# First attention of a two-layer network: queries stacked with their squares, and steps placed anew

## Chip, core and metric

The kernel runs on one core of a Trainium2 chip. The metric is the device time of one execution in microseconds, compared by the median of several runs.

## What is computed

Two layers, each an attention and a feed-forward with a residual and a layer norm after either. Only the first attention is touched, beside two placements at the end of the first feed-forward. It is a linear attention with random features over 4 batches of 2048 rows, 16 heads of 16:

```python
proj = einsum('bhld,md->bhlm', x, orf) / d_k ** 0.25          # x is q or k, m = 64
norm = sum(x * x, axis=-1, keepdims=True) / (2 * sqrt(d_k))
phi  = (exp(proj - norm) + 1e-6) / sqrt(64)
kv, ksum = einsum('bhlm,bhld->bhmd', k_phi, v), sum(k_phi, axis=2)
out  = (q_phi @ kv) / (q_phi @ ksum)
x    = layernorm(x + out @ Wo.T + bo)
```

The feed-forward after it quantizes its weights and its inputs to 4 bits in blocks of 16; the weights are prepared during the first attention. A softmax attention and a routed feed-forward follow, unchanged.

## The kernel before

`make_plan` writes one list of steps. Each engine's program walks through this list and takes the steps that it has a function for, in the list's order; semaphores hold it where it needs another engine's result. Each engine is thus an in-order queue, and where a step stands in the list sets what it waits behind.

**Data.** The 8192 rows are 16 chunks C of 512 rows, 4 per batch b. For a chunk of keys the steps are k (two products with halves ht of 128 columns of Wk), v, phi (features of the keys, 4 per chunk) and kv (sums over the rows, 16 per batch); at the end of a batch kvs and kvt turn the sums into the matrices kvV and kvD (four copies on VectorE, L1467 to L1470). k of the next batch waits for these copies (`dve_kvt`).

**Queries** (`queries_order`): q(C, ht) is a product of 4 records, whose result ScalarE writes to qT with the bias (L1239); GpSimd squares it into q2 (L1800). pq(C, ht, g) makes the features of 4 heads in two banks: for k in 0, 1 a product of 32 rows of Wblk (the random features) with qT, and then for k in 0, 1 a product of 32 rows of Nblk (-1/8 for each head's block) with the squares, added in the same banks. ScalarE takes the exponential (L1248) and GpSimd adds 1e-6 and scales (L1805). The text calls that instruction the epsilon. num(C, ht) makes denominators in bank 7 and numerators in bank 4; VectorE takes the reciprocal (L1481) and multiplies into aT (L1486). o(C, g) is the output product, which VectorE adds to the residual X (L1493). res(C) is GpSimd's addition of the output bias to X (L1780). st0 takes the statistics (L1418, L1422), GpSimd makes rstd of them (L1813, L1815), and ap0 applies the norm (four instructions, L1429).

**Order.** The keys of batch 0 run alone (`keys_order(0)`), then the queries of batch b beside the keys of batch b + 1 (`beside_queries`, which puts so many key units behind each query step, 12 for a chunk). In the last batch there are no keys: two streams of queries, chunks 12 and 14 and chunks 13 and 15, alternate, and a third prepares the first two input groups of the feed-forward (`inputs_order`: qx, a quantization on VectorE; xa on ScalarE; xb, four instructions over 1024 columns on GpSimd, L1862 to L1869). The second stream has its own banks and buffers (`way`).

**Weights** (`weights_order`) of the feed-forward, for each of three matrices m: wl loads it, wq quantizes (five VectorE instructions over up to 1536 columns), wa (ScalarE) and wb (three of VectorE) round, and six wt transpose on TensorE through bank 7, which num and o also use. 81 steps with their blanks, one beside each query step.

**End of the feed-forward.** While its last tiles run, the first maxima (M on TensorE into two banks, MR a reduction on VectorE of 1.16 us, L1574) of the softmax attention are taken; 32 of them make row (0, 0), from which scores can start. The load xc2 (step pl, SP's queue) brings rows for the preparation of batch 1, whose transposes (pt) stand on TensorE's queue among the maxima.

In the records of TensorE all products have line L744 and all transposes L747. A float32 product leaves two records per instruction.

Of the kernel before, what the change touches and what calls it, by code (L numbers as in the profile page):

```python
# [12 lines left out]
ALU = mybir.AluOpType  # L13
# [48 lines left out]
def queries_order(b, chunks, way):  # L62
    stats = None
    for c in chunks:
        C = 4 * b + c
        yield [("q", C, 0)]
        yield [("q", C, 1), ("fq", C)]
        for ht, g in ((0, 0), (0, 1), (1, 0)):
            yield [("pq", C, ht, g)]
        yield [("num", C, 0)] + ([("ap0", stats)] if stats is not None else [])  # L70
        yield [("pq", C, 1, 1)]
        yield [("num", C, 1), ("res", C)]
        yield []
        for g in range(2):
            yield [("o", C, g)] + ([("st0", C)] if g else [])
        stats = C
    yield []
    yield [("ap0", C)]


def beside_queries(plan, b, keys, weights):

    behind = {"q": (1, 2), "pq": (1, 1, 1, 2), "num": (0, 3), "o": (1, 0)}
    for units in queries_order(b, range(4), 0):
        plan += units + next(weights, [])
        for name, C in (u[:2] for u in units if u[0] in behind):
            at = sum(u[:2] == (name, C) for u in plan)
            for _ in range(behind[name][at - 1]):
                plan += next(keys, [])

# [17 lines left out]
def inputs_order(G):  # L108

    for step in (("qx", G), ("xa", G), ("xb", G, 0), ("xb", G, 1), ("xb", G, 2), ("xb", G, 3)):  # L110
        yield [step]
        yield []
# [108 lines left out]
def make_plan():  # L221
# [57 lines left out]
    together(plan, queries_order(3, (0, 2), 0), queries_order(3, (1, 3), 1), chain(inputs_order(0), inputs_order(1)))  # L279
# [13 lines left out]
    for T in range(-1, NT + 7):  # L293
# [23 lines left out]
        if T == NT + 3:  # L317
            plan.append(("ap1", NT - 8))
        if T == NT:
# [17 lines left out]
    plan += [("pl", 1, 0), ("phase2",)]  # L337
# [113 lines left out]
def program(nc, t, ctx):  # L451
# [73 lines left out]
    qT = [take(f"qT{i}", [P, 2, 512]) for i in range(2)]  # L525
    q2 = take("q2", [P, 2, 512])
# [8 lines left out]
    way = ({"q2": q2, "rB": rB, "phq": phq, "banks": (4, 5, 7)},  # L535
           {"q2": k2[0], "rB": phi[1][:, 512:1024], "phq": vq, "banks": (0, 1, 3)})
# [125 lines left out]
    for e, o in enumerate((0, 8192, 24576, stack_at, 4096, 12288, 16384, 28672)):  # L662
# [27 lines left out]
    (pool_setup, pool_res, pool_k2, pool_phi, pool_q, pool_pq, pool_eps, pool_eps1, pool_rstd, pool_shift, dve_wr, pool_qx,  # L690
     pool_ps, pool_R2, pool_at) = (sem(n) for n in (
        "pool_setup", "pool_res", "pool_k2", "pool_phi", "pool_q", "pool_pq", "pool_eps",
# [47 lines left out]
    def tensor_program(eng):  # L740
# [102 lines left out]
        def q(C, ht):  # L843
# [3 lines left out]
            if ht:  # L847
                w.wait_ge(act_q, at["q", C, 0])
# [9 lines left out]
        def pq(C, ht, g):  # L858
            i, (b4, b5, b7) = C % 2, way_of(C)["banks"]
            w.wait_ge(act_q, at["q", C, 1])  # L860
            w.wait_ge(dve_setup, 4)
# [8 lines left out]
            w.wait_ge(pool_q, at["q", C, 1])  # L870
            for k in range(2):

                s, c = slice(32 * (2 * g + k), 32 * (2 * g + k) + 32), slice(P * (2 * g + k), P * (2 * g + k) + P)
                mm(bank(b5 + k), Wblk[s, c], qT[i][s, ht, :], True, False)
            for k in range(2):
                s, c = slice(32 * (2 * g + k), 32 * (2 * g + k) + 32), slice(P * (2 * g + k), P * (2 * g + k) + P)
                d = mm(bank(b5 + k), Nblk[s, c], way_of(C)["q2"][s, ht, :], False, True)
            d.then_inc(pe_pq, 1)

        def num(C, ht):  # L880
# [20 lines left out]
            else:  # L901
                w.wait_ge(act_q, at["q", C, 1])
# [270 lines left out]
    def scalar_program(eng):  # L1173
# [59 lines left out]
        def q(C, ht):  # L1233
# [5 lines left out]
            eng.activation(qT[C % 2][:, ht, :], bank(b4), ACT.Identity, bias=bqk["q"][:, ht:ht + 1], scale=1.0).then_inc(act_q, 1)  # L1239
# [157 lines left out]
    def vector_program(eng):  # L1397
# [34 lines left out]
        def setup():  # L1432
# [5 lines left out]
            eng.memset(W[:, 1280:1536], 0.0).then_inc(dve_setup, 1)  # L1438

# [20 lines left out]
        def kvt(b):  # L1460
# [9 lines left out]
            eng.tensor_copy(Dn[64:128, :, 16:32], kv[64:128, :, 16:32]).then_inc(dve_kvt, 1)  # L1470

# [287 lines left out]
        stages = {"setup": setup, "wq": wq, "wb": wb, "bo": bo, "kvt": kvt, "num": num, "o": o, "st0": st0,  # L1759
# [8 lines left out]
    def pool_program(eng):  # L1768
# [23 lines left out]

        def q(C, ht):
            w.wait_ge(act_q, at["q", C, ht])
            if former(C) is not None:
# [446 lines left out]
```

## Time and profile before

| | us |
|---|---|
| median of 3 runs | 4654.1 |
| their range | 4651.65 to 4659.11 |
| the profiled execution | 4639.76 |
| its span | 4637.7 |
| TensorE busy in the span | 4385.2 (95%) |
| VectorE busy | 3396.8 (73%) |
| ScalarE busy | 2794.6 (60%) |
| GpSimd busy | 1012.4 (22%) |

PE is TensorE's products, PEld its weight loads, DVE is VectorE, ACT ScalarE, POOL GpSimd, SP the engine that issues most DMAs. PEclk is the mean granted clock of TensorE as a share of its full speed. A row of the timeline has the start, the length, the engine, the line, the operation with output and inputs, a count, and in brackets how long the engine stood idle before it and for whom. The first attention takes the first 690 us of the span, the first feed-forward lasts until 1340 us.

### The profile page before, as it was taken

What the parts mean: (1) busy time and instruction counts of PE and PEld (TensorE: products, weight loads), DVE (VectorE), ACT (ScalarE), POOL (GpSimd) and SP (SyncE); (2) the same over time, 40 slices, a digit from 0 to 9 for tenths busy, and PEclk for the clock granted to TensorE, in tenths of its full rate; (3) what the DMA queues carried; (4) which work ended last, traced back from release to release, by engine and by line L of the source; (5) the groups of instructions that cost most, each with busy time, mean ns of one, the idle gap of its engine ahead of it and who ended that gap; (6) DMA issues with size and microseconds to landing.
All of it is one profiled execution on the core that took longest, in us unless ns stands there. A gap on an engine that the chain in (4) does not pass through costs nothing.

```text
span 4637.7 us, 66610 instructions
## 1 busy us (share of the span) xinstructions
PE 4385.2 (95%) x26073; PEld 1670.4 (36%) x26076; DVE 3396.8 (73%) x3722; ACT 2794.6 (60%) x5273; POOL 1012.4 (22%) x989
## 2 busy tenths in 40 slices
PE   9988979999979999999999999999999999999895
PEld 5544536666642222222222222222222232222285
DVE  1443368877977788888778888777888988888332
ACT  3332323333326788887777778777777767787621
POOL 3443453445311200001121010221111001000223
PEclk9999989999989999999999999999999999999998
DMA  3111000021213321122332311333222122222232
GB/s 103 34 34 55 19 20 5 28 73 62 103 53 95 105 93 42 65 77 72 113 105 72 98 57 71 119 95 110 63 77 83 46 72 59 73 77 77 74 116 54
DMA packets 230278, 330.52 MB, mean 71 GB/s; under 512 B 36870, under 2 KB 171464, under 8 KB 227912
## 3 DMA queue, kind: packets, MB, share of 16 engines
q1 hardware_dynamic: 227084, 318.40, 20.9%
q0 software_dynamic: 2880, 7.87, 0.9%
q8 instruction: 205, 3.36, 0.3%
q14 instruction: 109, 0.89, 0.1%
HBM read 218.71 MB, written 98.04 MB: 68 GB/s over the span
## 4 chain that ended last, share of the span: by engine, by line
PE 67%; DVE 11%; POOL 3%; DMA 2%; issue 2%; ACT 1%; SPq 1%; POOLq 0%; DVEq 0%; another core or an unknown queue 0%; ACTq 0%
PE ps L744 66%; DVE mx L1574 4%; PE ps L747 2%; DVE stat L1418 1%; DMA pk<-Ob 1%; DVE hn L1412 1%; DVE hn L1553 0%; DVE hn L1548 0%; DMA KS<-kd 0%; DMA rd<-pk 0%; SPq L2058 0%; DVE eb L1429 0%; DMA QS<-mrow 0%; DMA ypar<-eo,tabs 0%; ACT Pb L1340 0%
## 5 line engine op out<-in xcount | busy, mean ns | idle before, releaser
L1574 DVE TENSOR_REDUCE mx<-ps 128x1 f32<-128x1024 f32 x2048 | 2407.4, 1219 | 434.3 <-PE ps L744 431.1
L1340 ACT ACTIVATE Pb<-ps 128x512 f32<-128x512 f32 x4096 | 2202.4, 597 | 521.0 <-PE ps L744 516.8
L744 PE MATMUL ps<-QS,KS 98*128 98x512 bf16 x4096 | 1249.4, 386 | 15.6 <-ACT Pb L1340 7.4
L744 PE MATMUL ps<-Pb,VA 128*32 128x512 f32 x8192 | 1096.9, 608 | 0.1
L744 PE MATMUL ps<-KM,QM 64*128 64x512 bf16 x4096 | 658.1, 388 | 48.5 <-DVE mx L1574 46.7
L744 PEld LDWEIGHTS ps<-QS,KS 98*128 98x128 bf16 x4096 | 260.2, 98 | 1087.7 <-ACT Pb L1340 904.4
L744 PEld LDWEIGHTS ps<-KM,QM 64*128 64x128 bf16 x4096 | 179.9, 93 | 603.9 <-issue 351.8
L744 PEld LDWEIGHTS ps<-Pb,VA 128*32 128x32 f32 x8192 | 161.4, 108 | 400.5 <-issue 399.5
L1887 POOL CAST mrow<-mres 16x128 bf16<-16x128 f32 x64 | 17.9, 279 | 1293.0 <-ACT mres L1177 1293.0
L1481 DVE RECIPROCAL rB<-ps 128x512 f32<-128x512 f32 x28 | 94.0, 3356 | 262.0 <-PE ps L744 261.7
L744 PE MATMUL ps<-wdT,hT 128*128 128x256 f32 (+1 forms) x768 | 194.3, 395 | 15.6 <-DVE X L1559 14.2
L744 PE MATMUL ps<-wgT,xqT 128*128 128x352 f32 x512 | 170.2, 477 | 0.0
L1820 POOL TENSOR_TENSOR den<-Ob,den 128x512 f32<-128x512 f32 x64 | 81.4, 1272 | 396.4 <-DMA den<-rd 396.4
L744 PEld LDWEIGHTS ps<-wdT,hT 128*128 128x128 f32 (+1 forms) x768 | 141.2, 193 | 68.5 <-issue 42.8
L744 PE MATMUL ps<-wuT,xqT 128*128 128x352 f32 x512 | 161.9, 459 | 0.0
L1813 POOL TENSOR_SCALAR vpe<-mv 128x4 f32<-128x4 f32 (+1 forms) x52 | 14.9, 286 | 607.9 <-DVE mv L1422 607.7
L1876 POOL CAST parts<-pres 128x1024 bf16<-128x1024 f32 x32 | 37.6, 1176 | 460.6 <-ACT pres L1177 431.1
L1198 ACT ACTIVATE phi<-ps 128x1024 f32<-128x1024 f32 x64 | 65.5, 1024 | 119.3 <-PE ps L744 119.3
L1532 DVE TENSOR_TENSOR hh<-ps,sg 128x704 f32<-128x704 f32 x64 | 56.5, 882 | 92.7 <-PE ps L744 88.4
L1177 ACT ACTIVATE pres<-ps 128x512 f32<-128x512 f32 x64 | 38.1, 597 | 132.2 <-PE ps L744 110.2
L744 PEld LDWEIGHTS ps<-wuT,xqT 128*128 128x128 f32 x512 | 97.6, 191 | 54.6 <-issue 0.7
L1248 ACT ACTIVATE phq<-ps 128x1024 f32<-128x1024 f32 x56 | 57.3, 1023 | 98.5 <-PE ps L744 98.5
(238 smaller groups left out, 4415.7 us busy)
## 6 DMA issues: line engine op xcount, KB each, us to landing
QM<-qd SPq DMA_DIRECT2D x128, 256.0 KB
KM<-kd SPq DMA_DIRECT2D x128, 256.0 KB
qd<-parts SPq DMA_DIRECT2D x96, 256.0 KB, 2.8
kd<-parts SPq DMA_DIRECT2D x96, 256.0 KB, 2.8
QS<-qd SPq DMA_DIRECT2D x64, 384.0 KB
KS<-kd SPq DMA_DIRECT2D x64, 384.0 KB
vdr<-vst SPq DMA_DIRECT2D x64, 256.0 KB, 2.8
den<-rd SPq DMA_DIRECT2D x64, 256.0 KB
```

What stands on the lines that cost most here:

```text
L744: return eng.matmul(out, a, b, start=start, stop=stop, skip_group_check=skip)
L747: return eng.transpose(out, a, ident[0:n, 0:n])
L1177: return eng.activation(out, a, ACT.Copy, bias=0.0, scale=1.0)
L1198: eng.activation(phi[n % 3], bank(1, 2), ACT.Exp, bias=0.0, scale=1.0).then_inc(act_phi, 1)
L1248: eng.activation(flat(way_of(C)["phq"][ht][:, 2 * g:2 * g + 2, :]), bank(b5, 2), ACT.Exp, bias=0.0, scale=1.0).then_inc(act_pq, 1)
L1340: eng.activation(Pb[(u - 1) % 9], o, ACT.Exp, bias=0.0, scale=0.25).then_inc(act_A, 1)
L1412: eng.tensor_tensor(blk(xn), blk(x), wide(rs, n // 16, 16), ALU.mult).then_inc(own, 1)
L1418: d = eng.bn_stats(stat[:, i % 4, j, :], x[:, j, :])
L1481: eng.reciprocal(f["rB"], bank(b7)).then_inc(dve_rec, 1)
L1532: eng.tensor_tensor(hh[p % 2][:, 704 * b:704 * b + 704].rearrange("p (a b) -> p a b", a=2), bank(2, 2).rearrange("p (a b) -> p a b", a=2)[ ...
L1574: eng.tensor_reduce(mx4[qc % 2][:, 4 * i + q, h:h + 1], o, AX, ALU.max).then_inc(dve_D, 1)
L1820: eng.tensor_tensor(den, Ob, den, ALU.mult).then_inc(pool_at, 1)
```

## The change

- The query matrix and its bias are permuted on the host, so that a product's result has the heads of group g = 0 and g = 1 in alternating blocks of 32 partitions. ScalarE writes it twice, to qs[0] and qs[1]; VectorE then overwrites in each the 32-partition blocks of the other group with squares (128 instructions in all). A matrix Wq4, built at the start by eight copies on VectorE, holds the matching rows of Wblk and Nblk. pq is then two products of 64 rows. GpSimd's squares, q2 and their semaphores go.
- `queries_order`: ap0 of a chunk stands with the next chunk's pq(C, 0, 0), also from one batch to the next, and only in the last batch at the end; res stands with pq(C, 0, 1).
- Weights: their steps begin at the thirteenth step of the keys of batch 0 and run on beside the queries, except behind the first num of a chunk. w0 and bo move up.
- `inputs_order` loses its blanks.
- The load pl(1, 0) moves ahead of the end of the feed-forward, and preparation steps start only when 12 maxima are in the list.

```diff
-        for ht, g in ((0, 0), (0, 1), (1, 0)):
-            yield [("pq", C, ht, g)]
-        yield [("num", C, 0)] + ([("ap0", stats)] if stats is not None else [])
+        yield [("pq", C, 0, 0)] + ([("ap0", stats)] if stats is not None else [])
+        yield [("pq", C, 0, 1), ("res", C)]
+        yield [("pq", C, 1, 0)]
+        yield [("num", C, 0)]
         yield [("pq", C, 1, 1)]
-        yield [("num", C, 1), ("res", C)]
+        yield [("num", C, 1)]
...
-    yield []
-    yield [("ap0", C)]
+    if b == 3:
+        yield []
+        yield [("ap0", C)]
...
-    for units in queries_order(b, range(4), 0):
-        plan += units + next(weights, [])
+    for units in queries_order(b, range(4), 4 * b - 1 if b else None):
+        plan += units
...
+        if not units or units[0][0] != "num" or units[0][2]:
+            plan += next(weights, [])
...
     for step in (("qx", G), ("xa", G), ("xb", G, 0), ("xb", G, 1), ("xb", G, 2), ("xb", G, 3)):
         yield [step]
-        yield []
...
-    together(plan, keys_order(0))
-    plan.append(("bo",))
     plan.append(("w0",))
+    for i, units in enumerate(keys_order(0)):
+        plan += units + (next(w, []) if i > 11 else [])
+        if i == 11:
+            plan.append(("bo",))
...
-    together(plan, queries_order(3, (0, 2), 0), queries_order(3, (1, 3), 1), chain(inputs_order(0), inputs_order(1)))
+    together(plan, queries_order(3, (0, 2), 11), queries_order(3, (1, 3), None), chain(inputs_order(0), inputs_order(1)))
...
+        if T == NT + 4:
+            plan.append(("pl", 1, 0))
...
-    plan += [("pl", 1, 0), ("phase2",)]
+    plan.append(("phase2",))
...
-        if len([u for u in plan if u[0] == "M"]) % 2 == 0 and ("mx", 0, 0) not in plan:
+        made = len([u for u in plan if u[0] == "M"])
+        if made % 2 == 0 and made > EARLY + 2 and ("mx", 0, 0) not in plan:
             background()
...
             if ht:
-                w.wait_ge(act_q, at["q", C, 0])
+                w.wait_ge(act_q, 2 * at["q", C, 0])
...
-            w.wait_ge(pool_q, at["q", C, 1])
+            w.wait_ge(dve_q2, 2 * at["q", C, ht] - 1 + g)
             for k in range(2):
 
-                s, c = slice(32 * (2 * g + k), 32 * (2 * g + k) + 32), slice(P * (2 * g + k), P * (2 * g + k) + P)
-                mm(bank(b5 + k), Wblk[s, c], qT[i][s, ht, :], True, False)
-            for k in range(2):
-                s, c = slice(32 * (2 * g + k), 32 * (2 * g + k) + 32), slice(P * (2 * g + k), P * (2 * g + k) + P)
-                d = mm(bank(b5 + k), Nblk[s, c], way_of(C)["q2"][s, ht, :], False, True)
+                d = mm(bank(b5 + k), Wq4[64 * k:64 * k + 64, g, :], qs[i][g][64 * k:64 * k + 64, ht, :])
...
-            eng.activation(qT[C % 2][:, ht, :], bank(b4), ACT.Identity, bias=bqk["q"][:, ht:ht + 1], scale=1.0).then_inc(act_q, 1)
+            for g in range(2):
+                eng.activation(qs[C % 2][g][:, ht, :], bank(b4), ACT.Identity, bias=bqk["q"][:, ht:ht + 1], scale=1.0).then_inc(act_q, 1)
...
+            w.wait_ge(ld_n, 16)
+            w.wait_ge(dve_setup, 4)
+            for j in range(4):
+                s, c = slice(32 * j, 32 * j + 32), slice(P * j, P * j + P)
+                eng.tensor_copy(Wq4[s, j % 2, :], Wblk[s, c])
+                d = eng.tensor_copy(Wq4[s, 1 - j % 2, :], Nblk[s, c])
+            d.then_inc(dve_blk, 1)
...
+        def q(C, ht):
+            for g in range(2):
+                w.wait_ge(act_q, 2 * at["q", C, ht] - 1 + g)
+                for k in range(2):
+                    o = 64 * k + 32 * g
+                    x = qs[C % 2][g][o:o + 32, ht, :]
+                    d = eng.tensor_tensor(qs[C % 2][g][64 * k + 32 - 32 * g:64 * k + 64 - 32 * g, ht, :], x, x, ALU.mult)
+                d.then_inc(dve_q2, 1)
...
-        def q(C, ht):
-            w.wait_ge(act_q, at["q", C, ht])
-            if former(C) is not None:
-                w.wait_ge(pe_pq, at["pq", former(C), 1, 1])
-            else:
-                w.wait_ge(pe_phi, 64 if C else 0)
-            x = qT[C % 2][:, ht, :]
-            eng.tensor_tensor(way_of(C)["q2"][:, ht, :], x, x, ALU.mult).then_inc(pool_q, 1)
```

## Rows read from the trace of the kernel before

**Rows 1.** Windows of batches 1 to 3: length, busy us (count) by engine, PEclk, DMA share, GB/s.
```profile
249.10:420.70 171.60, 154.71 (x1240) 83.99 (x1238) 63.50 (x92) 53.68 (x69) 68.66 (x60) 0.96 0.17 54
420.70:579.90 159.20, 148.21 (x1219) 81.05 (x1220) 54.82 (x86) 48.91 (x57) 64.34 (x60) 0.99 0.07 21
579.90:690.00 110.10, 84.07 (x352) 39.22 (x350) 66.12 (x89) 23.54 (x26) 56.15 (x43) 0.81 0.03 11
```

**Rows 2.** Groups by shape, 0 to 690 us: count, busy us, mean ns, idle before.
```profile
L744 PE MATMUL ps<-q,Nblk 32*128 32x512 f32 x224 | 60.5, 617 | 0.0
...
L1805 POOL TENSOR_SCALAR phq<-phq 128x1024 f32<-128x1024 f32 x56 | 58.4, 1043 | 110.3 <-ACT phq L1248 110.3
```

**Rows 3.** Waits: TensorE from 86 us (us, times, longest); last row VectorE from 0.
```profile
PE ps L744 <- DVE kvD L1470: 13.1, 3, 4.6
...
PE ps L747 <- DVE rB L1481: 6.7, 4, 2.6
...
DVE kvV L1467 <- PE ps L747: 74.2, 1, 74.2
```

**Rows 4.** Timeline, batch 1: start us, us, engine, line, operation, count, idle before.
```profile
400.46 0.60 PE L744 MATMUL ps<-Nblk,k 64*128 64x256 f32 x4
...
400.89 0.60 PE L744 MATMUL ps<-Wblk,kT 64*128 64x256 f32 x4
...
401.85 1.13 PE L744 MATMUL ps<-qT,Wblk 32*128 32x512 f32 x4
...
402.81 1.02 PE L744 MATMUL ps<-q,Nblk 32*128 32x512 f32 x4
...
403.77 0.65 PE L744 MATMUL ps<-phi,va 128*32 128x64 f32 x32
```

**Rows 5.** Timeline: a query copy, the q product after it, and two-input SBUF instructions of VectorE.
```profile
339.46 0.69 ACT L1239 ACTIVATE qT<-ps,bq 128x512 f32<-128x512 f32 x1 [3.72 <-PE ps L744]
...
340.20 1.98 PE L744 MATMUL ps<-xq,WqT 128*128 128x512 f32 x4 [0.19 <-ACT qT L1239]
...
1299.83 1.63 DVE L1412 TENSOR_TENSOR hn<-hh,hs 128x1408 f32<-128x1408 f32 x1
...
588.18 1.22 DVE L1412 TENSOR_TENSOR fq<-X,fs 128x1024 f32<-128x1024 f32 x1
...
636.19 2.00 DVE L1412 TENSOR_TENSOR fq<-X,fs 128x1024 f32<-128x1024 f32 x1
```

**Rows 6.** Timeline at the end of batch 2: ap0, and TensorE after the copies.
```profile
582.64 2.09 DVE L1429 TENSOR_SCALAR X<-X,mv,rstd 128x256 f32<-128x256 f32 x4 [1.47 <-POOL rstd L1815]
...
585.99 6.42 PE L744 MATMUL ps<-xq,WqT 128*128 128x512 f32 x8 [4.57 <-DVE kvD L1470]
...
587.83 0.34 PEld L744 LDWEIGHTS ps<-xq,WqT 128*128 128x128 f32 x1 [0.52 <-issue]
```

**Rows 7.** Timeline, batch 0: the o product behind a quantization and a reciprocal.
```profile
123.46 3.38 PE L744 MATMUL ps<-WoT,aT 128*128 128x256 f32 x8 [3.26 <-DVE aT L1486]
```

**Rows 8.** Timeline, batch 3: the wait for squares, ap0 beside GpSimd's instructions.
```profile
640.22 2.08 PE L744 MATMUL ps<-qT,Wblk 32*128 32x512 f32 x4 [3.79 <-POOL q L1800]
...
664.90 4.72 POOL L1780 TENSOR_TENSOR X<-X,bo 128x1024 f32<-128x1024 f32 x2
...
665.90 8.64 DVE L1429 TENSOR_SCALAR X<-X,mv,rstd 128x256 f32<-128x256 f32 x4
...
682.09 0.76 DVE L1486 TENSOR_TENSOR aT<-ps,phi 128x256 f32<-128x256 f32 x2
```

**Rows 9.** Timeline, end of the feed-forward: last add, xc's load, and who waited.
```profile
1339.72 0.42 DVE L1559 TENSOR_TENSOR X<-ps,X 128x256 f32<-128x256 f32 x1 [1.21 <-PE ps L744]
...
1346.64 0.51 SPq L2029 DMA_DIRECT2D xc<-x1d  x1
...
1351.17 1.12 PE L747 MATMUL ps<-identity,xc 128*128 128x128 f32 x4 [10.36 <-DMA xc<-x1d]
...
1352.87 4.62 DVE L1574 TENSOR_REDUCE mx<-ps 128x1 f32<-128x1024 f32 x4 [8.63 <-PE ps L744]
```

More of the change, by code:

```diff
@@ L59, in keys_order, with queries_order @@
     yield [("kvt", b)]
-def queries_order(b, chunks, way):
-    stats = None
+def queries_order(b, chunks, stats):
     for c in chunks:
@@ L524, in program @@
     k2 = [take(f"k2{i}", [P, 2, 512]) for i in range(2)]
-    qT = [take(f"qT{i}", [P, 2, 512]) for i in range(2)]
-    q2 = take("q2", [P, 2, 512])
+    qs = [[take(f"qs{i}_{g}", [P, 2, 512]) for g in range(2)] for i in range(2)]
+    Wq4 = take("Wq4", [P, 2, P])
     va = [take(f"va{i}", [P, 4, 16, 32]) for i in range(2)]
@@ L534, in program @@
     vq = [v.rearrange("p a b c -> p (a b c)").rearrange("p (a b) -> p a b", a=4) for v in va]
-    way = ({"q2": q2, "rB": rB, "phq": phq, "banks": (4, 5, 7)},
-           {"q2": k2[0], "rB": phi[1][:, 512:1024], "phq": vq, "banks": (0, 1, 3)})
+    way = ({"rB": rB, "phq": phq, "banks": (4, 5, 7)},
+           {"rB": phi[1][:, 512:1024], "phq": vq, "banks": (0, 1, 3)})
     way_of = lambda C: way[C in (13, 15)]
@@ L859, in pq @@
             i, (b4, b5, b7) = C % 2, way_of(C)["banks"]
-            w.wait_ge(act_q, at["q", C, 1])
-            w.wait_ge(dve_setup, 4)
+            w.wait_ge(dve_blk, 1)
             if C == 0:
@@ L901, in num @@
             else:
-                w.wait_ge(act_q, at["q", C, 1])
+                w.wait_ge(act_q, 2 * at["q", C, 1])
             for k in range(4):
@@ L1757, in yn @@
             norm_apply(xr[g][:, 5 * f:5 * f + 5, :], ("yp", g, f), 5)
-        stages = {"setup": setup, "wq": wq, "wb": wb, "bo": bo, "kvt": kvt, "num": num, "o": o, "st0": st0,
+        stages = {"setup": setup, "wq": wq, "wb": wb, "bo": bo, "kvt": kvt, "q": q, "num": num, "o": o, "st0": st0,
                   "ap0": ap0, "fold": fold, "qx": qx, "up": up, "qa": qa, "qb": qb, "qc": qc, "da": da, "st1": st1,
@@ L1929, in ys @@
                     in_=xr[g][:, b, :], in_offset=None, bounds_check=8191, oob_is_err=False).then_inc(st_fin, 16)
-        stages = {"setup": setup, "res": res, "k": k, "phi": phi_, "q": q, "pq": pq, "st0": st0, "st1": st1, "st2": st2,
+        stages = {"setup": setup, "res": res, "k": k, "phi": phi_, "pq": pq, "st0": st0, "st1": st1, "st2": st2,
                   "yp": yp, "of": of, "xb": xb, "ps": ps, "oe": oe, "R2": R2, "gx": gx,
@@ L2173, in layout @@
     kt = lambda w, n: f(np.asarray(w).T.reshape(-1, P, n).transpose(1, 0, 2).reshape(P, -1))
+    mid = np.arange(D).reshape(2, 2, 2, 32).transpose(0, 2, 1, 3).reshape(-1)
     for n in "qkvo":
-        a[f"W{n}T"] = kt(inputs[f"L0_attn_W{n}"], D)
+        a[f"W{n}T"] = kt(np.asarray(inputs[f"L0_attn_W{n}"])[mid if n == "q" else slice(None)], D)
     for n in "qk":
-        a[f"b{n}"] = f(np.asarray(inputs[f"L0_attn_b{n}"]).reshape(2, P).T)
+        a[f"b{n}"] = f(np.asarray(inputs[f"L0_attn_b{n}"])[mid if n == "q" else slice(None)].reshape(2, P).T)
     a["bo"] = f(np.broadcast_to(np.asarray(inputs["L0_attn_bo"]).reshape(1, D), (P, D)))
```

4 lines of the change are left out of this document (2 added, 2 removed).

## Prediction

> **What bounds the kernel now.** I read the windows first, cut where the first query product of each batch starts [rows 1]. In the second and third batch TensorE is busy 90 and 93% of the time while VectorE, ScalarE and GpSimd are at 31 to 40%, so here TensorE's instructions are the time, plus its waits. In the last 110.1 us, which hold the fourth batch, TensorE falls to 76%, at a mean granted clock of 0.81, and VectorE is at 60%: this stretch is a chain through several engines. Then the groups by shape [rows 2]: the norm product of the queries (Nblk with the squares) has 224 records (32 more read their squares from a key buffer); it is a product of its own, as long as that of the features. Third the waits [rows 3]: TensorE for the copies of the key-value sums (kvD) 13.1 us, for a reciprocal ahead of weight transposes 6.7. Last the timeline of single places. The feed-forward stage after 690 us isn't touched but for two placements at its end.
>
> **Part 1: one product for features and norm.** One pq step starts at 401.85, its norm half at 402.81, the next unit at 403.77 [rows 4]: 0.96 us for the features, 0.96 for the norms. In either half two 32-row products, 4 records of 512 columns, run side by side. The new step has two 64-row products. Does such a pair run side by side too? The keys' products show it: 4 records of 64 rows and 256 columns in the 0.43 us from 400.46 to 400.89 [rows 4], half the columns in half the time. So a pq step costs 0.96 instead of 1.92. In the three TensorE-bound batches: 48 steps x 0.96 = 46.1 us at full clock, 47 at the mean granted clock of 0.98 [rows 1]. The last batch's 16 steps (15 us) lie in the chain and are counted in part 5. Bounds of the product: 0 (pairs in series) to 0.96 a step.
>
> **Part 2: what makes the stacked queries.** ScalarE writes each result twice: 32 more activations x 0.687 = 22 us [rows 5], on an engine a third busy. But the second query product, q(C,1), reuses the bank and waits for both copies, 0.69 us later than now. The key unit between covers it when it is a 1.9 us product (first chunk of a batch) and not when it is a small kv unit (the other three), where q(C,1) already starts on the first copy's end (340.20 after 339.46 + 0.69 [rows 5]). 9 x 0.69 = +6. The squares leave GpSimd (32 instructions, no price: it doesn't bound there) for VectorE: 128 instructions over 32 partitions. None of that form is in the trace. Two-input SBUF rows take 1.63 us for 1408 elements and 1.22 for 1024 [rows 5], a slope of 1.06 ns, so 512 elements take 0.68; the lower bound is 0.55 (by that slope alone), the upper 1.1 (the 1024 row beside GpSimd took 2.00, 1.64 times 1.22 [rows 5]). I take 0.68: 128 x 0.68 = 87 us, 5.4 per chunk of some 37. In the first three batches this is beside TensorE: a square starts when ScalarE is done, VectorE has the residual add and 1.8 us of statistics ahead of it and is then free, and pq(C,0,0) follows q(C,1) and two key units, some 5.7 us after the first copy, where the first pair of squares needs 1.4. Without that cover each chunk would pay what is left. ScalarE's second copies also stand ahead of the keys' exponentials: +1 per batch, between 0 and 2, taken as +3. The 8 block copies at the start fall where VectorE is idle.
>
> **Part 3: the norm of a batch's last chunk (ap0).** At the end of a batch VectorE does statistics, waits for GpSimd's rstd, applies the norm (2.09 us [rows 6]), and only then copies the sums; k(C,0) waits for these: TensorE is idle 4.57 us and resumes at half speed, 8 records of the query product take 6.42 us [rows 6] where 4 take 1.98 at full speed [rows 5], and a weight load of 0.34 us follows a pause of 0.52 [rows 6], 0.86 for a record of 512 columns. There are three such waits, 13.1 us together [rows 3]. With ap0 behind the next chunk's squares, the copies come right after the statistics; the wait falls from 4.6 to about 1.1, as the query product before it ends 1.1 us before the copies would. 3 x 3.5 = 10.5, and the slow clock behind it (6.42 less 3.96 is 2.5 here, about 2 on the mean) 3 x 2: -16 together. ap0 moves to where VectorE is free. What is queued behind it there is num's reciprocal, 5 us later.
>
> **Part 4: weights.** The batches with weight steps last 171.6 (second) and 159.2 us (third) [rows 1]: 12.4 us for 10 or so transposes which are 0.6 of product each; the rest is waiting. The transposes wait for the reciprocal on bank 7 (6.7 us in 4 waits [rows 3]) and for residual adds. In the first batch a quantization of 1536 columns stood ahead of a reciprocal, whereupon TensorE sat 3.26 us and then took 3.38 us for 8 records of 256 columns, half speed [rows 7]. Now a weight step is taken in 41 of the first batch's key steps, where bank 7 is free and VectorE idle (74.2 us without a break [rows 3]), and none right behind the first num. By count the whole sequence of 81 ends in batch 0. Gone: about -7 of bank waits and -5 of the aT stall; new: the third quantization lies between o(1,0) and o(1,1), whose add frees the bank of the next q, so +3. Net -9, bounds -14 and 0. The first loads (w0, the weights, bo) are issued earlier on SP's queue, ahead of some x loads; SP's next waits are for products of TensorE, so nothing late is put ahead. bo's product now stands at key step 11, whose turn comes long after the loads at the start: no price. The x add of GpSimd (res, 2.36 us each, 4.72 for two [rows 8]) moves behind pq(C,0,1)'s epsilon, ahead of pq(C,1,0)'s: that one is needed two units later, no price.
>
> Parts 1 to 4: -47 + 6 + 3 - 16 - 9 = -63, with [-75, -40].
>
> **Part 5: the last batch.** Two chunks run together. From the copies to the end of the last aT (585.99 less the 0.15 of a signal [rows 6]) it takes now 97 us (682.09 + 0.76) [rows 8]. I lay the new order out by engine. Chunks 12 and 13: the input quantization (qx, then xb) has lost its blank steps, so GpSimd gets four xb (SBUF passes over 1024 columns, each about as long as a res) and two res among its epsilons (1.04 each [rows 2]); the seventh and eighth epsilon come some 22 us after the first. The first reciprocals come 2 us sooner, the last two 5 us later than now: +5. Chunks 14 and 15: GpSimd no longer owes xb or squares. The wait for squares (3.79 us [rows 8]) goes, so does most of the slow clock behind it; VectorE has 16 squares (10.9 us) and two ap0 ahead of the reciprocals. Laid end to end from the last aT of the first pair: 40 us instead of 60. But ap0 took 8.64 us beside the big GpSimd instructions [rows 8] where it takes 2.09 otherwise [rows 6], and it now falls beside res: +6. So -20 + 5 + 6 = -9, with [-20, +8].
>
> **Part 6: end of the feed-forward.** xc2 is loaded after the last x1d store, at 1346.64; TensorE is idle 10.36 us for it and VectorE 8.63 [rows 9]. The load moves to where the last dn is done (its add starts at 1339.72 [rows 9]), and lands in 4.5 us as now. Maxima go on until 12 are made before the first preparation step, so VectorE goes on from 1344.24 (1352.87 less 8.63). Row (0,0) needs VectorE for all 32 maxima, so its idle 8.63 us are the price: -9 with what the slow clock after the idle time costs, bounds -14 and -4. The preparation steps put off come later beside the main loop, which has room for them well ahead of batch 1's first use.
>
> **The sum.** -63 - 9 - 9 = -81. The profiled execution took 4639.8 us (span 4637.7 and 2.1 around it): 4559 by the sum. The median of the runs is 4654.1, 0.3% above it; the times are compared by medians, so I forecast 4654.1 - 81 = 4573.
>
> **Rivals.** (a) *The port between VectorE and GpSimd.* ap0's 8.64 us and the 2.00 for 1.22 [rows 5, 8] show that the two hold each other up on SBUF operands. Were each pair of squares to wait for one epsilon (1.04 [rows 2]), the last batch would gain nothing (+6 instead of -9) and each of 12 chunks would start 1 us later: -81 + 15 + 12 = -54, 4600 us. Chance 20%.
> The Trainium skill (SBUF — State Buffer, "SBUF: two separate sides") speaks against moving squares to VectorE: an instruction with two SBUF inputs contends with GpSimd for an exclusive lock held for the whole instruction. By that rule the squares cost up to twice; the 2.00 us row agrees with it, and (a) is its time.
> (b) *More comes back*: fewer long waits, so the clock (0.96 in the second batch) stays at 1.0, and the last batch follows the laid-out order without +6. -81 - 8 - 12, about 4553. Chance 12%.
> (c) *The pair of 64-row products doesn't overlap*: a step stays at 1.9. The 47 go and the last batch gains 5 less: 4573 + 52 = 4625. Against it speak the keys' rows [rows 4]. Chance 3%.
> (d) *Slower*: the squares are late at every chunk. They stand on VectorE's in-order queue behind the add and statistics; if pq(C,0,0) waits over 3.3 us in all 16 chunks, and a half-speed stretch of 2 us follows each as in [rows 6], the 81 are lost (16 x 5.3 = 85). With squares 6 us late: 4573 + 128 = 4701. Now the cover is 5.7 us against 1.4, so VectorE would have to be 8 us behind. Chance 4%.
> Forecast 61%.
>
> **How the numbers follow.** Forecast's own range: 4573 with parts at their ends not all together, 4548 to 4595. To hold 8 in 10 I add case (a) and most of (b): 4545 to 4612. A change within 0.2% (9 us) can't be told from none here. Faster: (a), (b), (c), the forecast: 0.93, less a little for what I can't see: 0.92; same 0.03; slower 0.05.
>
> **What would show it.** Pq records of 64 rows, 4 per 0.96 us, and no second group; three kvD waits near 1 us; squares at 0.68 us; the third batch some 18 us shorter, the second about 31 (no weights left in it); the stretch from the copies to the last aT near 88 us; no DMA wait before the first transposes of xc. Wrong would make it: squares over 1 us, TensorE waiting for squares at chunk starts, a GpSimd queue that stays behind in chunks 12 and 13, or weights that stall the keys.

## The result and the profile after

| us | before | after |
|---|---|---|
| median of the runs (4 each) | 4652.9 | 4571.0 |
| their range | 4651.3 to 4659.1 | 4567.6 to 4578.1 |
| profiled execution's span | 4637.7 | 4569.3 |
| TensorE busy | 4385.2 | 4315.6 |
| VectorE busy | 3396.8 | 3491.5 |

The ratio is 0.9824, with a 95% interval of 0.9806 to 0.9841: 82 us faster, where 81 were forecast. In a later comparison (g_after below) it was 0.9846, 0.983 to 0.9862. The profiled execution of before lies 13 us under its median and that of after on its median, so the two spans differ by 68 us only. In these traces the stretch from the first score to the last product with V varies between 2992 and 3009 us and what follows it between 235 and 255, for one and the same kernel too (the two traces of the change: 2993.8 and 246.3, 2994.3 and 235.3). In the change's two traces the stages of the attention repeat to 1.3 us, its last batch to 0.1, and the reasons are read there. Batch 1 of before is less steady: in e4_end, whose plan is the same up to there, it takes 174.9 us instead of 171.7, at a mean granted clock of 0.94 instead of 0.96.

Stages of the traces in us, cut where the first query product of a batch starts (the fourth ends where its last residual add starts; [rows 1] cut it at 579.90, where that product starts at 579.5, hence 158.7 and 109.9 here); "chain" is the part of the fourth batch from the end of the kvD copies to the end of the last aT; "end" is from the last add of the feed-forward to the first score:

| kernel | start | batch 0 | batch 1 | batch 2 | batch 3 | chain | feed-forward | end |
|---|---|---|---|---|---|---|---|---|
| before | 83.6 | 165.5 | 171.7 | 158.7 | 109.9 | 97.0 | 650.4 | 65.3 |
| after | 84.9 | 152.0 | 139.6 | 139.6 | 106.8 | 98.1 | 651.5 | 54.8 |
| e1_old_products | 83.5 | 162.3 | 153.4 | 153.4 | 104.5 | 94.1 | 648.9 | 54.9 |
| e2_ap0 | 84.5 | 164.3 | 165.9 | 153.4 | 93.6 | 83.2 | 651.5 | 65.4 |
| e3_weights | 85.3 | 164.9 | 158.7 | 159.7 | 110.3 | 97.4 | 650.4 | 63.9 |
| e4_end | 83.2 | 164.1 | 174.9 | 159.4 | 110.1 | 97.2 | 650.4 | 54.8 |

Up to the first score the change gains 75.9 us: 63.4 before batch 3, 3.1 in it, 10.5 at the end, less 1.1 in the feed-forward. The chain itself is 1.1 us longer, what lies around it in batch 3 is 4.2 shorter.

The windows of batches 1 to 3, for [rows 1]: length, busy us (count) of TensorE, its weight loads, VectorE, ScalarE, GpSimd, the granted clock, DMA share, GB/s:

```profile
236.94:376.50 139.56, 130.31 (x1154) 75.07 (x1154) 74.73 (x117) 53.05 (x65) 56.49 (x52) 1.00 0.19 61
376.50:516.10 139.60, 130.31 (x1154) 75.09 (x1155) 74.78 (x117) 53.06 (x65) 56.47 (x52) 1.00 0.08 24
516.10:622.90 106.80, 72.65 (x288) 30.50 (x288) 98.54 (x121) 27.91 (x34) 53.09 (x34) 0.82 0.03 10
```

TensorE has 18 to 24 us less to do in batches 1 and 2, and the second no longer differs from the third. In the last batch TensorE went from 84 to 73 us and VectorE from 66 to 99 of 107: VectorE is nearly always busy there. The groups by shape, for [rows 2] (busy us, mean ns | idle before):

```profile
L1492 DVE TENSOR_TENSOR qs<-qs 32x512 f32<-32x512 f32 x128 | 103.4, 808 | 22.2 <-ACT qs L1245 19.9
L754 PE MATMUL ps<-qs,Wq 64*128 64x512 f32 x256 | 74.0, 667 | 17.3 <-ACT phq L1254 10.2 <-DVE qs L1492 7.1
L1245 ACT ACTIVATE qs<-ps,bq 128x512 f32<-128x512 f32 x64 | 40.5, 684 | 91.7 <-PE ps L754 91.7
```

The waits of TensorE from 86 us on, for [rows 3] (us in total, times, longest):

```profile
PE ps L754 <- DVE X L1516: 11.0, 11, 2.9
PE ps L754 <- DVE qs L1492: 7.1, 3, 3.5
PE ps L754 <- ACT qs L1245: 6.2, 9, 0.8
PE ps L754 <- DVE kvD L1483: 4.6, 4, 1.7
```

The nine waits for the second copies are the nine of part 2, with its 6.2 us; before, eight waits of 0.2 us stood there, 1.6 in all, so the second copies cost 4.6 more. The three waits for kvD that made 13.1 us are 0.98 each; the fourth, 1.7, is in batch 0, where TensorE had none before. The timeline of a feature step in batch 1, for [rows 4], and of the start of batch 2, for [rows 6]:

```profile
390.55 1.13 PE L754 MATMUL ps<-qs,Wq 64*128 64x512 f32 x4
391.51 0.60 PE L754 MATMUL ps<-Wblk,kT 64*128 64x256 f32 x4
...
376.54 1.96 PE L754 MATMUL ps<-xq,WqT 128*128 128x512 f32 x4 [0.66 <-DVE X L1516]
379.47 1.95 PE L754 MATMUL ps<-xk,WkT 128*128 128x512 f32 x4 [0.98 <-DVE kvD L1483]
```

The step takes 0.96 us, from 390.55 to 391.51, with its norms in it. TensorE waits 0.98 us for the copies and goes on at full speed. The end of the feed-forward, for [rows 9]:

```profile
1274.39 0.36 SPq L2043 DMA_DIRECT2D xc<-x1d  x1
...
1276.59 9.24 DVE L1597 TENSOR_REDUCE mx<-ps 128x1 f32<-128x1024 f32 x8
...
1279.51 1.11 PE L757 MATMUL ps<-identity,xc 128*128 128x128 f32 x4
```

The transposes of xc no longer wait for the load, and eight maxima run without a break where VectorE stood idle 8.63 us.

### The profile page after: what moved, and what is told of

Read it like the earlier page. It is cut to its first block, busy times and chain, and to the rows that moved or that the text cites. A ratio compares the mean times of both kernels' runs of the same rounds, so it can differ in the third digit from the quotient of the medians.

```text
span 4569.3 us, 66262 instructions
## 1 busy us (share of the span) xinstructions
PE 4315.6 (94%) x25817; PEld 1642.9 (36%) x25820; DVE 3491.5 (76%) x3858; ACT 2811.9 (62%) x5305; POOL 978.9 (21%) x957
## 4 chain that ended last, share of the span: by engine, by line
PE 68%; DVE 11%; DMA 3%; POOL 2%; issue 2%; ACT 1%; SPq 1%; POOLq 0%; DVEq 0%; another core or an unknown queue 0%; ACTq 0%
PE ps L754 66%; DVE mx L1597 4%; PE ps L757 2%; DMA pk<-Ob 1%; DVE stat L1424 1%; DVE hn L1418 1%; DMA x2d<-eb 1%; DVE qs L1492 0%; DVE hn L1576 0%; DMA rd<-pk 0%; DVE hn L1571 0%; DMA KS<-kd 0%; SPq L2072 0%; DVE eb L1435 0%; DMA QS<-mrow 0%
## 5 line engine op out<-in xcount | busy, mean ns | idle before, releaser
L1504 DVE RECIPROCAL rB<-ps 128x512 f32<-128x512 f32 x28 | 94.0, 3358 | 106.8 <-PE ps L754 106.7
L754 PE MATMUL ps<-wgT,xqT 128*128 128x352 f32 x512 | 171.7, 481 | 0.0
L754 PEld LDWEIGHTS ps<-wdT,hT 128*128 128x128 f32 (+1 forms) x768 | 140.6, 192 | 68.5 <-issue 42.9
L1492 DVE TENSOR_TENSOR qs<-qs 32x512 f32<-32x512 f32 x128 | 103.4, 808 | 22.2 <-ACT qs L1245 19.9
L1182 ACT ACTIVATE pres<-ps 128x512 f32<-128x512 f32 x64 | 38.2, 598 | 132.4 <-PE ps L754 110.3
```

The costliest lines, as they stand in the source:

```text
L754: return eng.matmul(out, a, b, start=start, stop=stop, skip_group_check=skip)
L1182: return eng.activation(out, a, ACT.Copy, bias=0.0, scale=1.0)
L1492: d = eng.tensor_tensor(qs[C % 2][g][64 * k + 32 - 32 * g:64 * k + 64 - 32 * g, ht, :], x, x, ALU.mult)
L1504: eng.reciprocal(f["rB"], bank(b7)).then_inc(dve_rec, 1)
```

## The experiments

**First round: which part gives what.** Four kernels on one chip, before at 4650.4 us. The ratios aren't the quotients of the medians (these are 0.9923 for e1 and 0.9965 for e3 and e4), so the gains in time are known to some 6 us only, and the stages above say more. e1 is the change with the old feature and norm products; its edit is to put back the lines of q2, of Nblk's product and of GpSimd's q that the diff takes out:

```diff
-                d = mm(bank(b5 + k), Wq4[64 * k:64 * k + 64, g, :], qs[i][g][64 * k:64 * k + 64, ht, :])
+                mm(bank(b5 + k), Wblk[s, c], qT[i][s, ht, :], True, False)
...
+                d = mm(bank(b5 + k), Nblk[s, c], way_of(C)["q2"][s, ht, :], False, True)
```

> Every placement of the change (norms, weights, inputs, res, the load), but the queries' features and norms as two products again, squared on GpSimd. My account of the change: the placements are worth 16 (norm), 9 (weights) and 9 (end of the feed-forward), so about 34 us of the 82, 4619 us, and the stacked product some 48; the second and third batch last about 152 us each, 13 more than with the stacked product. Rival, that VectorE's squares ate the gain of the last batch (they took 1.37 us each there for 0.68): then the stretch from the last kvD copy to the last aT is shorter here, about 85 us, than the 97 that both kernels show, and the time nearer to 4607. If the squares cost nothing there, that stretch stays at 97 or more.

Measured: 4614.7 us, ratio 0.9936 (0.9916 to 0.9957), the second and third batch at 153.4. The chain, 94.1, lies between the rival's 85 and the 97 of squares that cost nothing. Stacking alone is after less e1: -10.3, -13.8 and -13.8 us in batches 0 to 2, and +2.3 in batch 3 (chain +4.0).

e2 is before with the norm placed anew and nothing else:

```diff
-        for ht, g in ((0, 0), (0, 1), (1, 0)):
-            yield [("pq", C, ht, g)]
-        yield [("num", C, 0)] + ([("ap0", stats)] if stats is not None else [])
+        yield [("pq", C, 0, 0)] + ([("ap0", stats)] if stats is not None else [])
+        yield [("pq", C, 0, 1)]
+        yield [("pq", C, 1, 0)]
+        yield [("num", C, 0)]
...
-    yield [("ap0", C)]
+    if b == 3:
+        yield [("ap0", C)]
```

> The kernel before with the norm of a chunk behind pq(C,0,0) of the next, also across batches; nothing else. My account: three waits for the copies fall from 4.6 to 1.1 us and the half-speed stretch behind each (2 us) goes, so 16 us, 4637; the third batch lasts 153 to 154 us instead of 159.2, a boundary sooner. Rival: the half speed has another cause than the wait; then 10 us, 4643, and the q products at the start of the fourth batch still run at half speed.

Measured: 4623.9 us, ratio 0.9942 (0.9923 to 0.9961), so 27 us. The starts of the batches give some 15 of them (batches 0 to 2: -1.2, -5.8, -5.3; batch 3 around its chain: -2.5), and the chain of the last batch gives 13.8 more: 2.6 up to its first reciprocal, since TensorE is no longer at half speed behind the copies (12 records of the query product take 5.39 us there instead of 8.14), 1.7 up to the first one of chunks 14 and 15, and 9.4 among the last four. VectorE's timeline shows how these come, beside the 8.64 us of [rows 8]:

```profile
620.75 4.83 DVE L1430 TENSOR_SCALAR X<-X,mv,rstd 128x256 f32<-128x256 f32 x8
637.28 3.36 DVE L1482 RECIPROCAL rB<-ps 128x512 f32<-128x512 f32 x1 [11.70 <-PE ps L745]
```

All eight norm instructions stand where VectorE has 11.7 us to spare. Before, four stood ahead of the second reciprocal and four, the 8.64 us, ahead of the third. TensorE's waits in the fourth batch of before, not read before the prediction, say what that cost:

```profile
PE ps L744 <- DVE aT L1486: 14.6, 4, 11.1
```

One wait of 11.1 us, for an aT behind the norm. In e2 the longest such wait is 3.3.

e3 is before with the weights' steps, w0 and bo placed as in the change, e4 is before with pl(1, 0) and the preparation placed as in it:

```diff
+        if not units or units[0][0] != "num" or units[0][2]:
+            plan += next(weights, [])
...
+    for i, units in enumerate(keys_order(0)):
+        plan += units + (next(w, []) if i > 11 else [])
```

> The kernel before with the weights' steps (and w0, bo) begun beside the keys of batch 0; nothing else. My account: 9 us, 4644; the second batch falls from 171.6 to about 159 us like the third, the first batch gains little since it now holds the steps of two matrices. Rival: the keys of batch 0 pay for it; then the first query product starts 5 us or more later than 83.6 us and the time is 4649 or more.

```diff
+        if T == NT + 4:
+            plan.append(("pl", 1, 0))
...
+        if made % 2 == 0 and made > EARLY + 2 and ("mx", 0, 0) not in plan:
```

> The kernel before with the load of xc2 and the first preparation steps placed as in the change; nothing else. My account: the first score product comes 55 us after the last add of the feed-forward instead of 65, TensorE doesn't wait for the load: 9 to 10 us, 4643. Rival: the preparation steps put off are paid in the main loop; then the stretch from the first score to the last V product (2992 us) is longer by as much and the time is the same as before.

Measured: e3 4634.2 us, ratio 0.9971 (0.9958 to 0.9984), batch 1 from 171.7 to 158.7 and no other stage by over 2; e4 4634.2, ratio 0.9978 (0.9964 to 0.9993), the end from 65.3 to 54.8. The main loop doesn't visibly pay for the steps put off: 2994 us in e4, 2992 before. Of e3's 13.0 us in batch 1 some 5 are the clock and not waits, by an estimate from the granted clock (0.96 of 171.7 us and 0.99 of 158.7, so 6.9 us against 1.6 lost). Against e2, e1 adds the dense input blocks and the early res to the last batch (and the weights' placement, which alone left the chain at 97.4): its chain is 94.1 against 83.2. The two placements thus take back 10.9 of the 13.8 that the norm gave, by the difference of two kernels that also differ in the weights; the third round undoes them by themselves.

**Second round: the last batch, and the squares' cover.** One run each; before took 4644.4 us on that chip. f1 puts the blanks between the input blocks back, f2 the x blocks' addition of the last batch behind num(C, 1):

```diff
     for step in (("qx", G), ("xa", G), ("xb", G, 0), ("xb", G, 1), ("xb", G, 2), ("xb", G, 3)):
         yield [step]
+        yield []
```

> The changed kernel with the blanks in the input quantization of the last batch restored; nothing else. The last batch gained nothing (98.1 us from the last kvD copy to the last aT, 97.0 before), while the moved norm alone brought it to 83.2. My theory: the close order of the inputs fills GpSimd's queue ahead of the epsilons of chunks 12 and 13; with the blanks the third reciprocal no longer comes 8 us after the second but 4, and the stretch falls to about 89 us. Rival: only the squares cost (22 us for 16 of them); then the first four reciprocals come closer but the stretch stays at 95 or more, as GpSimd's xb then meets the squares of chunks 14 and 15.

```diff
-        yield [("pq", C, 0, 1), ("res", C)]
+        yield [("pq", C, 0, 1)] + ([("res", C)] if b < 3 else [])
...
-        yield [("num", C, 1)]
+        yield [("num", C, 1)] + ([("res", C)] if b == 3 else [])
```

> The changed kernel with res of the last batch back beside num(C,1); nothing else. Theory: two res of 2.4 us stand ahead of the epsilons on which num waits; the stretch from the last kvD copy to the last aT falls by 2 to 5 us from 98.1. Rival: no change in it, since xb and the squares decide.

f4 makes the last batch's squares over one column of 512:

```diff
-                    x = qs[C % 2][g][o:o + 32, ht, :]
+                    n = 1 if C > 11 else 512
+                    x = qs[C % 2][g][o:o + 32, ht, 0:n]
```

> The changed kernel with the squares of the last batch taken over 1 of 512 columns (the rest of the squares is left out there, so the output of those chunks is not the reference's). Theory: the 16 squares of chunks 14 and 15, 22 us, are on the chain; without them the stretch from the last kvD copy to the last aT falls from 98.1 to 78 to 82 us. Rival: GpSimd's queue decides; then it stays above 90.

| kernel | time | chain | its clock | reciprocals of chunks 12 and 13 after the copies | first one of chunks 14 and 15 |
|---|---|---|---|---|---|
| after | 4571.0 | 98.1 | 0.81 | 24.3, 28.5, 36.6, 40.9 | 81.2 |
| f1_blanks | 4582.1 | 95.4 | 0.86 | 24.7, 29.0, 33.2, 37.5 | 78.5 |
| f2_late_res | 4576.4 | 93.0 | 0.87 | 23.0, 27.2, 36.6, 40.9 | 76.1 |
| f4_one_column | 4583.3 | 88.8 | 0.88 | 16.8, 21.0, 34.9, 39.1 | 71.9 |

(Before: 20.0, 24.2, 28.5, 32.7 and 70.6, at a clock of 0.80.) The times hold the loop's variation of some 10 us and can't rank these; the chains can. Each of the three gives some of it back: 2.7, 5.1 and 9.3 us. That is f1's rival (95 or more) and not its 89, f2's theory, and neither of f4's two (78 to 82, above 90). What they act on is seen in the change's own timeline, on TensorE, VectorE and GpSimd in turn:

```profile
553.23 1.94 PE L754 MATMUL ps<-phq,kvD 128*32 128x512 f32 x8 [8.78 <-POOL phq L1819]
...
582.13 6.42 PE L754 MATMUL ps<-qs,Wq 64*128 64x512 f32 x16 [3.33 <-DVE qs L1492]
592.00 2.08 PE L754 MATMUL ps<-qs,Wq 64*128 64x512 f32 x4 [3.45 <-DVE qs L1492]
...
536.10 7.05 DVE L1435 TENSOR_SCALAR X<-X,mv,rstd 128x256 f32<-128x256 f32 x4
543.18 3.36 DVE L1504 RECIPROCAL rB<-ps 128x512 f32<-128x512 f32 x1
...
574.09 21.98 DVE L1492 TENSOR_TENSOR qs<-qs 32x512 f32<-32x512 f32 x16
...
537.07 2.36 POOL L1803 TENSOR_TENSOR X<-X,bo 128x1024 f32<-128x1024 f32 x1
...
547.70 2.34 POOL L1880 TENSOR_TENSOR fq<-fc,fq 128x1024 f32<-128x1024 f32 x1
550.11 1.93 POOL L1883 TENSOR_TENSOR fq<-fq,fs 128x1024 f32<-128x1024 f32 x1
552.13 1.05 POOL L1819 TENSOR_SCALAR phq<-phq 128x1024 f32<-128x1024 f32 x1
...
576.36 2.74 POOL L1880 TENSOR_TENSOR fq<-fc,fq 128x1024 f32<-128x1024 f32 x1
579.17 2.26 POOL L1883 TENSOR_TENSOR fq<-fq,fs 128x1024 f32<-128x1024 f32 x1
```

In chunks 12 and 13 the first reciprocal comes right behind the norm of chunk 11 (536.10 to 543.15), whose four instructions take 7.05 us beside res (537.07) and its neighbours for the 1.38 that they take alone. Then TensorE waits 8.78 us for the epsilon at 552.13, which stands behind two input blocks on GpSimd's queue; f1 spreads these, and its third and fourth reciprocals come 3.4 us sooner after the copies. In chunks 14 and 15 sixteen squares take 21.98 us instead of the 10.9 of sixteen at 0.68, while GpSimd is busy 18.26 of these 21.98, with two late input blocks (576.36, 579.17) among its work.

f5 makes each square of the first three batches twice, in order, to see how much room VectorE has there:

```diff
+                    if C < 12:
+                        eng.tensor_tensor(qs[C % 2][g][64 * k + 32 - 32 * g:64 * k + 64 - 32 * g, ht, :], x, x, ALU.mult).then_inc(dve_tw, 1)
+                        w.wait_ge(dve_tw, 4 * (at["q", C, ht] - 1) + 2 * g + k + 1)
```

> The changed kernel with every square of batches 0 to 2 made twice, one after the other. My prediction's step, that VectorE's squares lie beside TensorE there: the second and third batch stay at 139.6 us (to 141), though VectorE gets 8 times 0.7 us more a chunk. Rival: the squares are on the path at the start of each chunk; then each of the batches is longer by 4 times 1.4 to 2.8 us, 145 to 151.

Measured: 4618.0 us, and each of batches 1 and 2 at 153.3 instead of 139.6, above both readings (139.6 to 141, 145 to 151): 3.4 us per chunk on the mean for 5.5 us of squares, the clock's fall from 1.00 to 0.98 included. One chunk of the change, on VectorE:

```profile
421.52 2.79 DVE L1492 TENSOR_TENSOR qs<-qs 32x512 f32<-32x512 f32 x4 [0.55 <-ACT qs L1245]
424.35 1.38 DVE L1435 TENSOR_SCALAR X<-X,mv,rstd 128x256 f32<-128x256 f32 x4
433.35 3.36 DVE L1504 RECIPROCAL rB<-ps 128x512 f32<-128x512 f32 x1 [7.62 <-PE ps L754]
```

and the same chunk of f5_twice on VectorE, GpSimd and TensorE:

```profile
452.76 0.69 DVE L1494 TENSOR_TENSOR qs<-qs 32x512 f32<-32x512 f32 x1
453.48 1.41 DVE L1496 TENSOR_TENSOR qs<-qs 32x512 f32<-32x512 f32 x1
...
457.81 2.76 DVE L1494 TENSOR_TENSOR qs<-qs 32x512 f32<-32x512 f32 x1
460.60 1.42 DVE L1496 TENSOR_TENSOR qs<-qs 32x512 f32<-32x512 f32 x1
462.05 3.57 DVE L1436 TENSOR_SCALAR X<-X,mv,rstd 128x256 f32<-128x256 f32 x4
465.55 3.34 DVE L1508 RECIPROCAL rB<-ps 128x512 f32<-128x512 f32 x1
...
453.05 1.29 POOL L1818 TENSOR_SCALAR phi<-phi 128x1024 f32<-128x1024 f32 x1 [6.96 <-ACT phi L1204]
457.34 2.67 POOL L1807 TENSOR_TENSOR X<-X,bo 128x1024 f32<-128x1024 f32 x1
...
469.03 1.07 PE L755 MATMUL ps<-phq,kvD 128*32 128x512 f32 x8 [3.24 <-DVE rB L1508]
```

The change has 7.62 us to spare ahead of the reciprocal. Doubling adds 5.5 us of squares; but the squares now reach into the time in which GpSimd works (it starts at 453.05), and from there take 1.41, and 2.76 beside the 2.67 of the x block, and the norm takes 3.57 instead of 1.38. The last five squares and the norm thus cost 5.0 and 2.2 us more than alone, and the reciprocal comes late: TensorE waits 3.24 us, not for the squares but for the reciprocal behind them. Over the three batches (86 to 557.3 us) it waits 22.2 us for such reciprocals, in 8 waits, and 7.7 us for squares, in 7; in the change it waits for neither there. The square that starts at 457.81 ends at 460.57, 0.56 after GpSimd's x block at 460.01, as if it had begun when that ended. By the Trainium skill (SBUF — State Buffer, "SBUF: two separate sides") a VectorE instruction with two SBUF inputs and a GpSimd instruction that reads SBUF lock each other out for a whole instruction. The trace agrees. The prediction read that rule as a cost of "up to twice"; the 2.76 us are four times 0.68.

**Third round: a better last batch.** Five runs each on one chip, before at 4641.5 us. g_after is the change again, g_both has both placements of f1 and f2 undone in the last batch, and g_act_squares moves that batch's squares to ScalarE as well:

> The changed kernel once more, as the measure for the two beside it: 4571 us within 5, 1.8% under the kernel before. Its last batch takes 98 us from the packing of the keys' products to the last transposition.

> The changed kernel with two of its placements undone in the last batch alone: the blank places between the input blocks are back, and the x blocks for the residual are loaded after the second numerator again. Theory (GpSimd's queue and VectorE's squares get in each other's way there): the two gave 2.7 and 5.1 us of that stretch alone, together 6 to 8, so some 91 us, and the kernel 7 us faster, 4564. Rival (the same 5 us seen twice): 93 us, 4566. Rival (what the stretch gives comes back as waits in the score loop, 0.2% of noise aside): no difference from the changed kernel.

```diff
+            for g in range(2 if C > 11 else 0):
+                w.wait_ge(act_i, 2 * (at["q", C, ht] - 24) - 1 + g)
+                for k in range(2):
+                    s, r = slice(64 * k + 32 * g, 64 * k + 32 * g + 32), slice(64 * k + 32 - 32 * g, 64 * k + 64 - 32 * g)
+                    d = eng.activation(qs[C % 2][g][r, ht, :], bank(b4)[s, :], ACT.Square, bias=bqk["q"][s, ht:ht + 1], scale=1.0)
+                d.then_inc(act_q, 1)
```

> As the one above, and in the last batch the squares are made by ScalarE out of the product's bank right after the two copies, in place of VectorE out of SBUF. Theory (the squares on VectorE hold GpSimd's large instructions up and are held up by them): with the squares away from VectorE the stretch gave 9.3 us, and with the two placements undone it goes to some 82 to 86 us, the kernel to 4556. Rival (ScalarE now issues 96 more instructions of some 0.7 us, 16 of them times four per chunk in the last batch, ahead of the features' exponentials, and is what ends the waits there): the stretch stays at 91 us or grows to 100, 4564 to 4573.

The last kernel is g_both with f4's squares of one column, so it too leaves the norms of the last batch's queries out (one run, 4563.8 us against 4655.5 for before):

> The changed kernel with the two placements undone in its last batch (the stretch from the copies to the last transposition took 88.0 us so), and the squares of that batch over one of their 512 columns, so that the norms of its queries are left out; what is left of each is its waits and its issue. Without the placements undone this took 9.3 us off the stretch. Theory (the time of the squares on VectorE stands in the chain whatever GpSimd's order): 88.0 less 9, some 79 us. Rival (most of the 9.3 was the squares' collision with the large instructions that now fall elsewhere): 84 to 87 us.

| kernel | median (range) | ratio to before (95%) | chain | its clock |
|---|---|---|---|---|
| g_after | 4567.2 (4558.7 to 4572.8) | 0.9846 (0.983 to 0.9862) | 98.1 | 0.81 |
| g_both | 4555.6 (4549.6 to 4568.1) | 0.9821 (0.9802 to 0.984) | 88.0 | 0.86 |
| g_act_squares | 4557.7 (4553.3 to 4558.3) | 0.982 (0.9806 to 0.9834) | 88.9 | 0.85 |
| g_both_one_column | one run | | 74.9 | 0.93 |

The two placements together give 10.1 us of the chain, more than 2.7 and 5.1 added and near the 10.9 of the first round. The medians agree (11.6 less than g_after), though the intervals overlap. With them undone the longest waits for an epsilon and for squares are these, and the sixteen squares of the second pair take 15.85 us:

```profile
581.12 1.94 PE L755 MATMUL ps<-qs,Wq 64*128 64x512 f32 x4 [3.16 <-DVE qs L1493]
...
594.26 1.31 PE L755 MATMUL ps<-phq,kvD 128*32 128x512 f32 x8 [4.22 <-POOL phq L1820]
...
566.54 15.85 DVE L1493 TENSOR_TENSOR qs<-qs 32x512 f32<-32x512 f32 x16
```

Squares of one column then give another 13.1 us, above the 9 of the first reading and far above the rival's 1 to 4. In g_both the 32 squares take 29.5 us, 7.7 more than at 0.68 each, so at most 7.7 of the 13.1 can be their lengthening beside GpSimd: the squares stand in the chain themselves too, in this order of GpSimd's as well. Moving them to ScalarE gives none of it, neither the theory's 82 to 86 nor the rival's 91 or more. The group of the squares, VectorE's idle time ahead of a reciprocal, and TensorE's waits in g_act_squares say why:

```profile
L1255 ACT ACTIVATE qs<-ps,bq 32x512 f32<-32x512 f32 x32 | 21.7, 679 | 0.6
...
L1517 DVE RECIPROCAL rB<-ps 128x512 f32<-128x512 f32 x4 | 13.4, 3358 | 34.8 <-PE ps L756 34.6
...
PE ps L756 <- ACT phq L1265: 7.2, 2, 3.7
...
PE ps L756 <- ACT qs L1255: 6.9, 4, 2.3
```

VectorE now idles 34.6 us, but its 32 squares (32, not the 96 of the expectation) cost ScalarE the same 0.68 us each, and TensorE waits for ScalarE's squares and for the exponentials behind them.

## Why the prediction was right, and what made up for its failed part

Up to the first score the change gained 75.9 us where the sum had 81. Part 5 missed by 10 (+1.1 in the chain for -9). Parts 1 to 4 gave 67.6 for 63 and part 6 about what was said, which makes up for half of that; the other 6 us of the measured 82 lie in main loop and tail, which the change touches only by the preparation steps put off and which vary by some 10 (by g_after's ratio the whole gain is 71). That the forecast time was met to 2 us is luck; that it lay in the range isn't.

**Parts 1 and 2** were forecast at -38 for the three TensorE-bound batches (-47, +6, +3); stacking alone gave -37.9 there (after less e1). Pairs of 64 rows run side by side (0.96 us a step), the second copy costs 4.6 us net, and a square of 512 columns takes 0.71 us on average in these batches (68.5 us for 96; 0.68 alone). TensorE never waits for squares there.

**Part 3** said -16. The starts of the batches gave some 15, as counted, and the full speed behind the copies 2.6 more in the last chain, 17 to 18 by its own terms; but e2 is worth 27 to 28. The rest, some 9 to 11 us, is a wait that the prediction has no term for: it prices "ap0 took 8.64 us beside the big GpSimd instructions" as +6 in its new place, and doesn't say that in its old place, among the last reciprocals, it put an 11.1 us wait on TensorE. Part 5's 40 us, with the norms laid ahead of the reciprocals, hold that gain without naming it.

**Part 4** said -9 and named batch 1 as the place; e3's stages gave some -10.4 up to the last residual add, its ratio -13.5 us (-19.5 to -7.4). The transposes' waits for the reciprocal are gone in e3, but "the rest is waiting" was wrong for some 5 us of the 12.4 between the batches: those are the clock. **Part 6** said -9; the end gave -10.5, in e4 and in the change.

**Part 5** is the failed one: the chain was to fall from 97 to 88 and stood at 98.1, inside the bounds [-20, +8] and far from the -9. Its two halves by the timeline: the last reciprocals of chunks 12 and 13 come 8.2 us later than before (5 forecast) and the first 4.3 later (2 sooner forecast). The first waits on VectorE behind the norm of chunk 11, 7.05 us where 1.38 is its length alone, a collision that the prediction put (as +6) in chunks 14 and 15; the last ones are late because TensorE waits 8.78 us for an epsilon. From the last reciprocal of the first pair to that of the second it takes 53.1 us instead of 60.1, where 40 and then 46 with the +6 were laid out. The mis-sized terms are the 16 squares, put down at 10.9 us and 21.98 in fact, the claim that GpSimd "no longer owes xb" there, where two input blocks ran beside the first of these squares, and the claim that res "moves behind pq(C,0,1)'s epsilon [...] no price": in the last batch it has one, 5.1 us by f2. What the change did to this chain is thus 13.8 us gained by the norm's place and 10.9 and 4.0 lost by the two placements and the stacking.

**The rivals.** (a), the port between VectorE and GpSimd, was partly right, in the last batch: squares and norms are lengthened there beside GpSimd. How much of the chain that costs isn't separated; most of the gain was lost already in e1, which has no square on VectorE. In batches 0 to 2 squares and GpSimd's instructions hardly meet. (b) took a mean clock of 1.0 in batch 1: it came so, from 0.96, but batch 1 is 32 us shorter where the forecast's terms said 31, so its further 8 didn't come. (c) is refuted by the 0.96 us step. (d) put the danger at pq(C,0,0), with "VectorE would have to be 8 us behind". f5_twice shows the danger nearer: 5.5 us more on VectorE cost 3.4 a chunk, for the cover that runs out first is the one ahead of the reciprocal, and the collision with GpSimd uses it up faster than the squares' own length.

What stays open: how the 10 us by which main loop and tail vary come about, which no run here tells; by which of its three or so small waits the last batch's chain would be shortened next; and how much of each gain in that chain is the clock's. TensorE's mean granted clock in it goes with its length, from 0.80 (97.0 us, before) and 0.81 (98.1) over 0.87 (94.1, e1) to 0.92 (83.2, e2) and 0.93 (74.9, g_both_one_column): part of the time falls at the lower of its two levels (1.2 and 2.4 GHz), so fewer waits also bring faster products, and no run here separates the two.

## What to carry over

Cost an instruction that is moved to VectorE twice: at its length alone, and at its length beside what GpSimd does in that stretch. Here the second was twice the first, and that showed in the one stage where both engines were busy. When steps change place, list for the stage which is a chain its own waits first: a wait of 11.1 us, whose going gave e2 9 us or more, stood in a view that was read only for the other stages.

## What the runs showed of the hardware

A reciprocal that reads PSUM takes 3.34 to 3.36 us whether GpSimd is busy or not, while two-input and one-input SBUF instructions of VectorE beside it take two to five times as long (squares 0.68 to 1.41 and 2.76, four norms 1.38 to 3.57 and 7.05), and GpSimd's pass that adds 1e-6 over 128x1024 lengthens too, from 1.05 to 1.29 us. On ScalarE, out of PSUM, a square over 32 partitions takes 0.68 us, as long as a copy over 128 (0.684). Pairs of 64-row products of 512 columns take 0.96 us at full clock, as pairs of 32-row ones do.
